# Row-max steps moved from the last down product into groups 4 to 7 of an attention + feed-forward kernel

## The reference, cut to what matters

```python
xn = _layernorm(x, axis=-1)                      # x: (2, 2048, 256), fp32
x = x + _L0_attn_ref(xn, ...) + _L0_ffn_ref(xn, ...)

# attention: 16 heads of 16 channels, keys equal queries
z = _layernorm(x, ln1_g, ln1_b); q, k, v = jnp.split(z @ w_in.T + b_in, 3, axis=-1); k = q
scores = jnp.einsum('nhld,nhsd->nhls', q, k) * scale
attn = jax.nn.softmax(scores, axis=-1)
out = jnp.einsum('nhls,nhsd->nhld', attn, v)      # then @ w_out.T + b_out

# feed-forward: ternary weights (rounded w / mean|w|), width 1024
h = jax.nn.gelu(x @ _ternary(W1).T + b1, approximate=False)
out = h @ _ternary(W2).T + b2
```

## Time and profile before

| what | us |
|---|---|
| median of 3 runs (1389.69 to 1390.75) | 1389.82 |
| the profiled execution | 1389.26 |
| its span in the trace | 1387.4 |
| PE busy, DVE busy, ACT busy in the span | 1358.9, 1315.5, 1242.7 |

### The profile page before, as it was taken

One profiled execution on the slowest core, in us unless ns is written; L12 is line 12 of the kernel. 1 busy time (PEld: TensorE's weight loads), 2 busy tenths in 40 slices (PEclk: granted clock), 3 DMA queues, 4 the chain that ended last, 5 costly groups with the idle time before them and its releaser, 6 DMA issues.

```text
span 1387.4 us, 32041 instructions
## 1 busy us (share of the span) xinstructions
PE 1358.9 (98%) x13274; PEld 459.6 (33%) x13274; DVE 1315.5 (95%) x1354; ACT 1242.7 (90%) x2263; POOL 162.4 (12%) x376
## 2 busy tenths in 40 slices
PE   7999999999999999999999999999999999999999
PEld 5656643222222222222222222222222222222244
DVE  6888899999999999999999999999999999999935
ACT  5665659999999999999999999999999999999975
POOL 3222143000000000000000000000222200002200
PEclk8999999999999999999999999999999999999999
DMA  6332300001111101101111111011111101012122
GB/s 240 73 80 68 98 20 8 30 31 33 33 33 32 33 33 34 34 33 33 33 34 33 33 33 35 29 35 47 54 54 56 55 33 35 32 35 64 41 83 105
DMA packets 55866, 67.23 MB, mean 48 GB/s; under 512 B 33344, under 2 KB 38880, under 8 KB 55466
## 3 DMA queue, kind: packets, MB, share of 16 engines
q1 hardware_dynamic: 55146, 63.55, 14.5%
q10 hardware_dynamic: 576, 1.65, 0.3%
HBM read 41.29 MB, written 16.77 MB: 42 GB/s over the span
## 4 chain that ended last, share of the span: by engine, by line
DVE 71%; PE 24%; DMA 2%; ACT 1%; issue 1%; POOL 0%; SPq 0%; ACTq 0%; DVEq 0%
DVE part_max L944 68%; PE ps L405 6%; PE ps L419 3%; PE ps L1278 3%; PE ps L1194 3%; PE ps L375 3%; PE ps L1214 2%; PE ps L496 2%; PE ps L477 1%; DMA rows<-in_rows 1%; ACT w L1171 1%; PE ps L466 1%; DMA max_rows<-max_split 1%; DVE w L936 0%; PE ps L506 0%
## 5 line engine op out<-in xcount | busy, mean ns | idle before, releaser
L1171 ACT ACTIVATE w<-ps 128x512 f32<-128x512 f32 x2048 | 1109.6, 596 | 62.4 <-PE ps L466 16.4
L944 DVE TENSOR_REDUCE part_max<-ps 128x1 f32<-128x1024 f32 x1024 | 1160.6, 1209 | 3.9 <-PE ps L375 3.7
L405 PE MATMUL ps<-w,v_ones 128*32 128x256 f32 (+1 forms) x7688 | 627.1, 398 | 0.6 <-DVE resid L868 0.3
L419 PE MATMUL ps<-qry,key 50*128 50x512 f16 x1984 | 398.5, 386 | 7.9 <-ACT w L1171 7.0
L375 PE MATMUL ps<-qry,key 48*128 48x512 f16 x2048 | 393.4, 380 | 4.5 <-DVE part_max L944 4.4
L405 PEld LDWEIGHTS ps<-w,v_ones 128*32 128x32 f32 x7688 | 151.4, 108 | 310.9 <-issue 159.2
L419 PEld LDWEIGHTS ps<-qry,key 50*128 50x128 f16 x1984 | 98.0, 92 | 429.8 <-ACT w L1171 411.5
L375 PEld LDWEIGHTS ps<-qry,key 48*128 48x128 f16 x2048 | 99.9, 93 | 83.1 <-issue 15.5
L732 POOL COPY v_ones<-v_all 128x128 f32<-128x128 f32 x64 | 19.5, 305 | 748.8 <-PE ps L405 748.8
L1130 ACT ACTIVATE hidden<-ps,columns 128x512 f32<-128x512 f32 x64 | 41.3, 677 | 26.9 <-PE ps L1278 26.6
L1278 PE MATMUL ps<-x_parts,w_ternary 128*128 128x512 f16 x256 | 62.0, 380 | 0.9 <-ACT hidden L1130 0.9
(11 more groups left out here) (159 smaller groups left out, 480.1 us busy)
## 6 DMA issues: line engine op xcount, KB each, us to landing
key<-q_parts SPq DMA_DIRECT2D x62, 128.0 KB
qry<-q_parts SPq DMA_DIRECT2D x62, 128.0 KB
o_heads<-o_evacuated SPq DMA_DIRECT2D x31, 256.0 KB, 10.1
key<-q_parts SPq DMA_DIRECT2D x66, 64.0 KB
qry<-q_parts SPq DMA_DIRECT2D x66, 64.0 KB
resid<-in_x SPq DMA_DIRECT2D x8, 512.0 KB, 13.6
q_parts<-q_split SPq DMA_DIRECT2D x16, 256.0 KB, 2.5
out<-resid SPq DMA_DIRECT2D x7, 512.0 KB, 4.3
```

Source lines behind the costliest of these rows:

```text
L405: mm = eng.matmul(pv[32 * c:32 * c + 2 * D, c0:c1], vst[:, kb, :], prob[kb % 2][:, c * BANK + c0:c * BANK + c1], start=(kb == 0), stop=(kb ...
L419: eng.matmul(ring_bank(v, i, False), key[v][r:r + KROWS, kb * P:(kb + 1) * P], qry[v][r:r + KROWS, c * BANK:(c + 1) * BANK], start=True, s ...
L944: dve.tensor_reduce(part_max[h % 2][:, blk, side:side + 1], pa[a % 2], AX.X, ALU.max).then_inc(s_r, 1)
L1171: act.activation(prob[kb % 2][:, c * BANK:(c + 1) * BANK], ring_bank(k, i, last), ACT.Exp, scale=exp_scale).then_inc(s_e, 1)
```

## The change

The 8 steps of head 1 leave the last down product, and the 40 steps are spread anew:

- Groups 4, 5 and 6 have six steps: one in the down product of the group before (pass 0, after f = 5), and five after the hidden products f = 0, 1, 3, 5, 7. On DVE the first is reduced ahead of `add_ffn(g - 1, 0)`, and one more stands ahead of the fourth second hidden part.
- Group 7 has eight in its first down product (that of group 6), from pass 0 on: three in pass 0, four in pass 1, one in pass 2; and six after f = 1..6, as before. On DVE six of the eight are reduced ahead of `add_ffn(6, 0)` and two ahead of `add_ffn(6, 1)`.
- The last down product has none.

```diff
+        BETWEEN_FULL = (0, 1, 3, 5, 7)
+        DOWN_FULL = ((0, 5),)
+        DOWN_LAST = ((0, 3), (0, 5), (0, 7), (1, 1), (1, 3), (1, 5), (1, 7), (2, 3))
         BETWEEN_LAST = (1, 2, 3, 4, 5, 6)
         ROWS_AT = (2, 1, 1, 0)
+        ROWS_AT_FULL = (2, 1, 1, 1)
         ROWS_AT_LAST = (2, 2, 2, 0)
-        EARLY = 6
...
+                if g >= NG // NB:
+                    first_rows(len(DOWN_FULL))
                 add_ffn(g - 1, 0)
...
             g = NG - 1
-            first_rows(KF // 2)
+            early = sum(p < 2 for p, _ in DOWN_LAST) - 1
+            first_rows(early)
             add_ffn(g - 1, 0)
-            first_rows(EARLY - KF // 2)
+            first_rows(len(DOWN_LAST) - early)
             add_ffn(g - 1, 1)
             q_factors(g)
             results(g, first_rows)
-            first_rows(STEPS * AHEAD - 1)
             add_ffn(g, 1)
-            first_rows(1)
...
             for n in range(TG * KF - 3 * FILL):
                 next(last_down)
-                if n % 3 == 2:
-                    first_a()
```

More of the change, by code:

```diff
@@ L339, in attention_ffn @@
         BETWEEN = (0, 1, 3, 5)
+        BETWEEN_FULL = (0, 1, 3, 5, 7)
+        DOWN_FULL = ((0, 5),)
+        DOWN_LAST = ((0, 3), (0, 5), (0, 7), (1, 1), (1, 3), (1, 5), (1, 7), (2, 3))
         BETWEEN_LAST = (1, 2, 3, 4, 5, 6)
         ROWS_AT = (2, 1, 1, 0)
+        ROWS_AT_FULL = (2, 1, 1, 1)
         ROWS_AT_LAST = (2, 2, 2, 0)
-        EARLY = 6
         HALF_GROUPS = NG // NB // 2
         HALF_STEPS = NBLK // 2
-        assert HALF_STEPS + len(BETWEEN) * (NG - 1 - NG // NB) + EARLY + len(BETWEEN_LAST) == NA
+        FULL_STEPS = len(BETWEEN_FULL) + len(DOWN_FULL)
+        assert HALF_STEPS + FULL_STEPS * (NG - 1 - NG // NB) + len(DOWN_LAST) + len(BETWEEN_LAST) == NA + STEPS * AHEAD
         assert HALF_STEPS == len(BETWEEN) * HALF_GROUPS
@@ L928, in results @@
                     if rows:
-                        rows((ROWS_AT_LAST if g == NG - 1 else ROWS_AT)[i])
+                        rows((ROWS_AT_LAST if g == NG - 1 else ROWS_AT_FULL if g >= NG // NB else ROWS_AT)[i])
                     if g and i == 0:
@@ L1198, in down_products, with ffn_down @@
                             yield t, f
-            def ffn_down(g, between=None):
+            def ffn_down(g, between=None, places=()):
                 pe.wait_ge(s_g, KF * (g + 1))
-                for t, f in down_products(g, ((0, 2), (1,), (3,))):
-                    if between and t % 2 and f % 2:
-                        between()
+                passes = ((0, 2), (1,), (3,))
+                for t, f in down_products(g, passes):
+                    for p, tiles in enumerate(passes):
+                        if tiles[-1] == t and (p, f) in places:
+                            between()
             def abs_total(j):
@@ L1235, in factor_transposes, with group @@
                 mm.then_inc(s_ft, 1)
-            def group(g, between=None, between_down=None):
+            def group(g, between=None, places=(), places_down=()):
                 first = g == 0
@@ L1257, in group @@
                     values(g - 1, 1)
-                    ffn_down(g - 1, between_down)
+                    ffn_down(g - 1, between, places_down)
                 wait(pe, s_vd, 2 * g)
@@ L1291, in group @@
                         values(g, 0)
-                    if between and f in (BETWEEN_LAST if g == NG - 1 else BETWEEN):
+                    if f in places:
                         between()
@@ L1313, in first_a @@
             def first_a():
-                h, a = next(steps, (None, None))
-                if h is None:
-                    return
+                h, a = next(steps)
                 if h == 0 and a == 0:
@@ L1321, in first_a @@
                 a_step(pe, h, h, a)
-            def first_a_early(calls=iter(range(TG * KF // 4))):
-                n = next(calls)
-                if n < EARLY:
-                    first_a()
[L1328 to L1332, removed]
+            for g in range(1, HALF_GROUPS):
+                group(g)
+            for g in range(HALF_GROUPS, NG // NB):
+                group(g, first_a, BETWEEN)
+            pe.wait_ge(s_pad, 16 * (2 * ROT - 1))
+            for g in range(NG // NB, NG - 1):
+                group(g, first_a, BETWEEN_FULL, DOWN_FULL)
+            group(NG - 1, first_a, BETWEEN_LAST, DOWN_LAST)
             values(NG - 1, 1)
```

## The result

The changed kernel takes 1394.81 us (median of 10 runs, 1392.44 to 1395.24), the kernel before 1390.11 us in the runs beside it. The ratio is 1.0031, with a 95% interval of 1.0023 to 1.0039: slower by 0.31%, or 4.3 us. The forecast was +3.2 us, 1393.0. Put on the 1389.82 of the forecast, the ratio gives 1394.1 us, inside the stated range of 1389.6 to 1394.6; the new median itself lies 0.2 us above its upper end.

What follows compares the result with a forecast made beforehand. DVE's row maxima bound the head stage, PE groups 2 to 6, group 7 mixed. 2.55 + 2.75 + 0.58 + 2.3 - 5.0 = +3.2 us gave 1393.0 us, range 1389.6 to 1394.6.

Steps and rivals of the forecast that it cites:

- Groups 4 to 6 bounded by PE, a step at 0.425 us: Groups 4 to 6: PE bounds them, so six steps more at 0.425 us each cost +2.55 us.
- The load behind step 8: Group 4's down product: step 8 reached at 105.9, PE stands still until its columns are loaded, +2.75 us.
- the lag of 0.5 us: At the load in group 4: time from the last data to the waiting engine, taken as some 0.5 us.
- The clock: Rival: PE's stop of 2.75 us in group 4 halves its clock, some 2.4 us lost, 1395.4 us; chance 0.08.
- Group 7's first down product: Group 7: its first down product with eight steps lasts 10.9 us instead of 10.3, +0.58 us.
- POOL's adds: Rest of group 7: POOL's bias adds start earlier and block six two-operand DVE operations, +2.3 us (0 to 3.3).
- The last down product: Last down product without steps: the unbroken run of reductions starts sooner, -5.0 us, with DVE idle for about 4 us.
- The edge: Whole kernel: most likely time at the edge between within 0.2% (0.48) and slower by over 0.2%, above 1392.6 us (0.46).
- the unlisted 0.10: Whole kernel: chance of 0.10 held for outcomes not listed, half on each side of the forecast.

Runs made afterwards that it cites:

- e3: The changed kernel with the four query pieces of the load issued first and step 8 waiting for these alone: 1390.55 us, ratio 1.0001 to the kernel before.
- e8: The changed kernel with step 8 waiting for the four query pieces alone, but all four key pieces issued ahead of them: 1395.04 us, ratio 1.0031.
- e10: The kernel before with only step 8 moved early, into the middle of the down product in group 4: 1395.19 us, ratio 1.0035.
- e2: The changed kernel with POOL's bias adds held back until the first add of group 7's down product is done: 1392.57 us, ratio 1.0014.
- e9: The changed kernel with two key pieces loaded first, then the four query pieces step 8 waits for, then two key pieces: 1392.26 us, ratio 1.0016.
- e1: The changed kernel with group 4's step moved out of the down product to behind hidden product f = 6: 1390.83 us, ratio 0.9999.
- e5: The kernel before with 16 of POOL's 32 bias adds put ahead of head 0's split_max, no step moved: 1391.97 us, ratio 1.0012.
- e4: The changed kernel with the edits of e2 and e3 together: 1387.97 us, ratio 0.9983 to the kernel before.
- e6: e2 with two steps back in the last down product and none in the down products of groups 4 and 5: 1387.37 us, ratio 0.9979.
- e7: e6 with a third step in the last down product, after piece 15, and none in group 6's down product: 1388.17 us, ratio 0.9982.

## Why the prediction was right, and where it was off

- *Groups 4 to 6 bounded by PE, a step at 0.425 us*: right. 21.74 and 21.75 us, 21.74 forecast. DVE carried both further steps in each group without holding PE.
- *The load behind step 8*: the mechanism was right (a DMA ends the wait; e3, e8 and e10 show it), the size was not. The step is the term of 2.75 us, with 2.9 as its upper end. I took the last data at 108.1 from the one trace and held that nothing could move it. In the changed kernel data still moved in the window at 109.00, and step 8 started some 0.5 us later, at 109.62. The windows of the DMAs (length, granted clock, DMA share, GB/s):

```profile
108.75:109.00 0.25, 1.00 0.06 25
109.00:109.25 0.25, 1.00 0.03 8
```

  In the four kernels with the full wait (the change, e2, e8, e10) step 8 started at 109.62, 108.62, 109.45 and 109.01; with e9's shorter one at 108.11. SP issued the DMAs at the same times within 0.25 us in all of them. The change is not what moved the landing: e1 has no stop, and its last data moved in the window at 108.50. One trace gave one landing of a spread of about 1 us; the lag of 0.5 us was right, and I gave it a range, but not the landing.
- *The clock*: the rival with a chance of 0.08 came about, in part. It cost 1.5 us in the profiled run and not 2.4: the slow stretch lasted 3.4 us and not the 4.8 that I assumed, and its first 0.3 us fell into the stop. The chance was too small: of the three traces with a full stop in the changed order (3.47, 2.68 and 3.48 us) all have a slow stretch, and e10's with 2.85 has none. The row on which I leaned, a stop of 1.33 us at full clock, said little: in e5 the pause at that very place was 1.58 us, and a slow stretch followed. That the stop brings the slow stretch is an inference from where the stretches lie; what exactly brings it is open (last section).
- *Group 7's first down product*: +0.68 for a forecast of +0.58.
- *POOL's adds*: right. +2.1 for +2.3; held back, they give 2.4 by the ratios; and 16 of them early in the kernel before cost 1.3 to 1.7. The Trainium skill ("SBUF — State Buffer", "SBUF: two separate sides") has VectorE with two SBUF inputs and a GpSimd operation that reads SBUF exclude each other. The rows agree: 1.75 against 1.28 us beside the adds, and 1.28 again without them. They also agree with the page's other half ("Who interferes with whom"), that reductions are not touched: 1.13 us each beside the adds and away from them.
- *The last down product*: -5.3 for -5.0, with DVE idle for 3.5 us (2.89, 0.23 and 0.35).
- *The edge*: the forecast put 0.48 on "within 0.2%" and 0.46 on slower. The two terms that were too small, 0.7 and 1.5 us, are what carried the result well over the edge. In the medians it is 4.3 to 4.7 us, less than the 5.2 of the profiled pair. That not every run has the long stop and the slow clock would explain it, but is not shown: the others have no trace, and their mean clocks (0.993 to 0.996) don't tell, since the profiled run of e1 has 0.994 too with no slow stretch in group 4. So there is luck in the range: from 1393.0 to its upper end were 1.6 us, the two terms came out 2.2 us too small together, and the profiled pair alone, at +5.2, would lie outside.
- *Slips in the working*: from 105.9 to 108.1 are 2.2 us, not 2.1; half of the unlisted 0.10 is 0.05, where 0.06 stands for a gain; and a DMA share of 0.21 in a window of 0.25 us does not say at which 0.05 us the data ended, so the lag of 0.5 us was known to 0.25 only. None of them moves the forecast by more than that.

## What to carry to other kernels

When a step is moved forward, look up what it waits for, and when that lands in several runs, not in one: here a wait that had 5 us of room became a stop of 3 us, and issuing four of the eight DMAs first removed it. When work ends earlier, ask who starts on it: an engine off the critical path began over 10 us sooner and slowed the one on it, and one wait put it back. A fair idea (the bound engine's work moved to where it idles) gave some 2.5 us (e4), and two side effects took 6.7.

## What the runs showed of the hardware

- A stop of PE of 2.68 us was followed by a granted clock of 0.50 for about 3.4 us, one of 2.85 us in another kernel was not, and one of 1.97 us was not either. The same order of instructions can have the slow stretch in one run and not in another: PE pauses for 2.17 to 2.19 us ahead of its first down product in e3, e4, e6 and e7, and some 1.6 us behind that pause the clock falls in e6 and e7 and stays up in e3 and e4.
- Shorter stops can have it behind them too. In the 12 traces there are seven slow stretches behind the first 28 us, each 3.4 us long: three at the load (the change, e2, e8), two at 41 us (e6, e7), one at 197 us behind a pause of 1.58 us (e5) and one at 887 us behind one of 1.39 us (e1). What one costs depends on the place: 1.5 to 1.7 us in group 4, 0.9 in e5, 0.5 in e6 (64.16 us from the first down product to group 4, against 63.66 in e3 and e4). The windows of e6 (length, PE busy, granted clock, DMA share, GB/s):

```profile
41.00:42.00 1.00, 1.00 (x8) 0.58 0.00 0
42.00:43.00 1.00, 1.00 (x7) 0.50 0.00 0
...
44.00:45.00 1.00, 1.00 (x9) 0.71 0.00 0
```

- The slow stretch needs no idle PE to go on: in e8 it lay wholly behind the stop. The stop ended at 109.45, and the clock fell only at about 110.9 and rose at about 114.3. The windows of e8 (length, PE busy, granted clock, DMA share, GB/s):

```profile
110.50:111.00 0.50, 0.50 (x6) 0.86 0.00 0
111.00:112.00 1.00, 1.00 (x7) 0.50 0.00 0
...
114.00:115.00 1.00, 1.00 (x10) 0.86 0.00 0
```

- The hidden part in the earlier trace rows that met a running POOL operation got longer by the overlap less about 0.2 us (2.22 against 1.27 us for an overlap of 1.14). POOL waits for DVE as well: between the two hidden parts from 201.49 on an add gets its turn, and it takes 1.70 us where the median of the 32 is 0.74. The timeline of POOL, the change:

```profile
201.91 1.70 POOL L730 TENSOR_TENSOR resid<-resid,bias_row 128x256 f32<-128x256 f32 x1
```
